# Mixture-of-experts phase of a fused layer on one core: the expert's conditional chunk taken last instead of first

## What is computed

```python
x = x + attention(layernorm(x))
x = x + moe(layernorm(x))

def moe(hidden_states, gate_w, w1, w2, w3):     # E=8 experts, K=2, H=256, F=896
    probs = softmax(hidden_states @ gate_w.T)
    # each token goes to its two best experts; an expert takes at most
    # capacity = 320 tokens of each of the 4 sequences: up to 1280 rows in all
    dispatch = einsum('bsm,bsec->ebcm', hidden_states, dispatch_mask)
    h1 = einsum('ebcm,emh->ebch', dispatch, w1)
    h3 = einsum('ebcm,emh->ebch', dispatch, w3)
    expert_out = einsum('ebch,ehm->ebcm', silu(h1) * h3, w2)
    return einsum('ebcm,bsec->bsm', expert_out, combine_mask)
```

## Time and profile before

| | us |
|---|---|
| median of 3 runs | 896.36 (894.65 to 896.64) |
| profiled execution, its own time | 896.49 |
| its span, first to last instruction | 894.8 |
| TensorE busy | 846.2 |
| VectorE, ScalarE, GpSimd busy | 472.9, 489.2, 467.1 |

### The profile page before, as it was taken

The page is one execution under the profiler, slowest core; times in us unless marked ns, Lnnn a source line. Parts: engine busy times, 40 slices in busy tenths (PEclk is TensorE's granted clock), DMA queues, the critical chain, the costliest instruction groups (busy, mean ns, idle before and its releaser), DMA issues. The chain is left out here.

```text
span 894.8 us, 18307 instructions
## 1 busy us (share of the span) xinstructions
PE 846.2 (95%) x6791; PEld 705.4 (79%) x6791; DVE 472.9 (53%) x1173; ACT 489.2 (55%) x876; POOL 467.1 (52%) x497
## 2 busy tenths in 40 slices
PE   3999999999999999889999999999999999999995
PEld 2777777777777777779889889879789889889885
DVE  6788788788888766343441442442351443342430
ACT  4578787777777779263542443443452444453331
POOL 4434766777767675564337355237346137447014
PEclk9999999999999999999999999999999999999998
DMA  5852132112111121546116236025417024314013
GB/s 154 320 193 67 50 102 67 62 56 80 38 38 38 38 98 53 170 150 139 42 42 118 86 92 111 5 78 89 112 48 137 22 72 92 82 42 54 7 19 42
DMA packets 50465, 73.93 MB, mean 83 GB/s; under 512 B 5056, under 2 KB 42176, under 8 KB 50368
## 3 DMA queue, kind: packets, MB, share of 16 engines
q1 hardware_dynamic: 35488, 53.46, 18.0%
q0 software_dynamic: 14592, 19.18, 12.5%
q10 hardware_dynamic: 288, 0.01, 0.0%
HBM read 38.41 MB, written 34.22 MB: 81 GB/s over the span
## 5 line engine op out<-in xcount | busy, mean ns | idle before, releaser
L1540 POOL TENSOR_TENSOR wlo<-wraw,whi 128x448 fp32r<-128x448 f32 x84 | 107.1, 1278 | 201.5 <-ACT whi L1597 201.5
L1817 PE MATMUL p<-xh,whi 128*128 128x512 f32 (+1 forms) x504 | 190.4, 378 | 7.3 <-DVE xl L1716 4.7
L1819 PE MATMUL p<-xh,wlo 128*128 128x512 f32 (+1 forms) x504 | 189.7, 376 | 0.0
L1818 PE MATMUL p<-xl,whi 128*128 128x512 f32 (+1 forms) x504 | 189.3, 376 | 0.0
L1734 DVE TENSOR_TENSOR hid<-gated,p 128x512 f32<-128x512 f32 (+1 forms) x126 | 81.1, 644 | 204.3 <-ACT gated L1611 204.3
L1548 POOL DMA_INDIRECT out<-ysb,index x80 | 126.0, 1575 | 85.2 <-ACT ysb L1633 55.1
L1611 ACT ACTIVATE gated<-p 128x512 f32<-128x512 f32 (+1 forms) x126 | 70.8, 562 | 179.7 <-PE p L1819 179.7
L1837 PE MATMUL py<-whi,hh 128*128 128x256 f32 x469 | 135.1, 288 | 6.2 <-DVE hl L1742 3.1
L1839 PE MATMUL py<-whi,hl 128*128 128x256 f32 x469 | 132.8, 283 | 0.0
L1838 PE MATMUL py<-wlo,hh 128*128 128x256 f32 x469 | 132.5, 283 | 0.0
L1817 PEld LDWEIGHTS p<-xh,whi 128*128 128x128 f32 x504 | 94.7, 188 | 27.4 <-DVE xl L1716 5.4
(11 more groups left out here) (192 smaller groups left out, 1441.1 us busy)
## 6 DMA issues: line engine op xcount, KB each, us to landing
wraw<-in_w SPq DMA_DIRECT2D x24, 896.0 KB
disp<-wraw SPq DMA_DIRECT2D x16, 662.5 KB, 9.2
xtok<-disp SPq DMA_DIRECT2D x16, 530.0 KB, 4.5
x_ring<-in_x SPq DMA_DIRECT2D x16, 256.0 KB, 3.0
out<-x SPq DMA_DIRECT2D x16, 256.0 KB
xtok<-disp SPq DMA_DIRECT2D x8, 265.0 KB, 6.1
out<-ysb,index POOLq DMA_INDIRECT x80
disp<-row,slot_i POOLq DMA_INDIRECT x64
```

The costliest lines, as they stand in the source:

```text
L1540: nc.gpsimd.tensor_tensor(wlo[e.const % 2][m][:, cut], wraw[k][:, cut], whi[e.const % 2][m][:, cut].bitcast(F32), ALU.subtract).then_inc(w ...
L1817: nc.tensor.matmul(dst[:, 0:w], hi[m][:, wcut], xh[xcut], start=(kt == 0), stop=False)
L1818: nc.tensor.matmul(dst[:, 0:w], hi[m][:, wcut], xl[xcut], start=False, stop=False)
L1819: ins = nc.tensor.matmul(dst[:, 0:w], lo[m][:, wcut], xh[xcut], start=False, stop=(kt == KT - 1))
```

## The change

`chunk_order` becomes 1, 2, 0 for experts 0 to 6 and 0, 1, 2 for expert 7, which keeps its old code under the name `last`. On TensorE `step` (now experts 1 to 6) is: `up` 1, then one branch on whether there is a rest. In its arm stand `turn` bank 4, `up` 2, `down` of chunk 1, `up` 0; in the other `up` 2 and `down` of chunk 1, between two passings-over. Then come `last_chunk` and `down_rest`. ScalarE and VectorE follow, so both arms there hold the second chunk's work as well. `first` has only three tiles' `down` ahead of the branch instead of four; the fourth follows `up` 2 inside the arms. On GpSimd the adds follow `tile_order`, so those of the rest come last, and the first of them waits for the adds of the expert's first five tiles.

```diff
 def chunk_order(e):
-    return [EARLY, *(c for c in range(NCH) if c != EARLY)] if e.reg is None and e.const == 0 else list(range(NCH))
+    return [1, 2, 0] if e.const < E - 1 else [0, 1, 2]
...
-    def run(eng, first, step):
+    def run(first, step, last):
         first(At(0))
-        step(At(1))
-        for e in range(2, E):
+        for e in range(1, E - 1):
             step(At(e))
+        last(At(E - 1))
...
         def add(e, t):
...
             pool.wait_ge(rows_in[0], 16)
+            if q == ST - REST and t < REST:
+                added_before(pool, e, ST // 2)
...
-            early = tile_order(e)[:CHUNKS[EARLY][1]]
+            early = tile_order(e)[:CHUNKS[EARLY][1] - 1]
...
-            for t in range(ST):
+            for q, t in enumerate(tile_order(e)):
                 add(e, t)
-                if t == ST - 3 and (e + 1).valid(E):
+                if q == ST - 3 and (e + 1).valid(E):
                     keep_index(e + 1)
...
     def on_scalar(act):
+        def with_rest_where_taken(e, between):
+            def hidden_rest():
+                turn_hi(e, TB - 1)
+                between()
+                hidden(e, 0, [])
+            def no_rest():
+                between()
+                n = chunk_at(e, 0) * FT
+                pass_over(act, e, (xh_ready, TB - 1, TB, 1), (gated_ready, n, HPE, FT), (hh_ready, n, HPE, FT))
+            where_taken(act, e, COMMON, hidden_rest, no_rest)
...
+        def step(e):
+            pieces = [(m, q) for m in range(3) for q in range(WP)]
+            half = pieces[FT - 1:]
+            hidden(e, 1, pieces[:FT - 1])
+            def second():
+                hidden(e, 2, list(half))
+                scale_chunk(e, 1)
+            with_rest_where_taken(e, second)
+            last_chunk(e, True)
+            scale_rest(e, 0)
...
     def on_vector(dve):
...
         def step(e):
+            hidden(e, 1)
+            with_rest_where_taken(e, lambda: hidden(e, 2))
+            next_rows(e + 1)
...
     def on_tensor(pe):
+        def with_rest_where_taken(e, between):
+            def up_rest():
+                turn(e, TB - 1)
+                between()
+                up(e, 0)
+            def no_rest():
+                pass_over(pe, e, (turned, TB - 1, TB, 1))
+                between()
+                pass_over(pe, e, (h_done, chunk_at(e, 0) * FT, HPE, FT))
+            where_taken(pe, e, COMMON, up_rest, no_rest)
...
         def first(e):
             t0, n = CHUNKS[EARLY]
-            for t in range(t0, t0 + n - 1):
+            for t in range(t0, t0 + n - 2):
                 down(e, t)
             for i in range(2, TB - 1):
                 turn(e, i)
-            down(e, t0 + n - 1)
+            down(e, t0 + n - 2)
             pe.wait_ge(taken_ready, 1)
-            rest_where_taken(e)
-            up(e, 2)
-            down_rest(e, 0)
+            def second():
+                up(e, 2)
+                down(e, t0 + n - 1)
+            with_rest_where_taken(e, second)
             last_chunk(e)
+            down_rest(e, 0)
         def step(e):
-            rest_where_taken(e)
             up(e, 1)
-            down_rest(e, 0)
-            up(e, 2)
-            down_chunk(e, 1)
+            def second():
+                up(e, 2)
+                down_chunk(e, 1)
+            with_rest_where_taken(e, second)
             last_chunk(e)
+            down_rest(e, 0)
```

More of the change, by code:

```diff
@@ L1519, in step @@
                 load_weights(nxt, 2)
-        run(sp, step, step)
+        run(step, step, step)
     def on_gpsimd(pool):
@@ L1578, in step @@
             added_before(pool, e, 0)
-            for t in range(ST):
+            for q, t in enumerate(tile_order(e)):
                 add(e, t)
-                if t == ST - 3 and (e + 1).valid(E):
+                if q == ST - 3 and (e + 1).valid(E):
                     keep_index(e + 1)
-        run(pool, first, step)
+        run(first, step, step)
         added_before(pool, At(E), 0)
@@ L1683, in first, with last @@
                 turn_hi(e, i)
-            scale_out(e, t0 + n - 1)
+            scale_out(e, t0 + n - 2)
             act.wait_ge(taken_ready, 1)
+            def second():
+                hidden(e, 2, [(m, q) for m in range(3) for q in range(WP)], 2)
+                scale_out(e, t0 + n - 1)
+            with_rest_where_taken(e, second)
[9 more added lines that the diff above has]
+            with_rest_where_taken(e, second)
+            last_chunk(e, True)
+            scale_rest(e, 0)
+        def last(e):
             rest_where_taken(e)
-            pieces = [(m, q) for m in range(3) for q in range(WP)]
-            hidden(e, 2, pieces, 2)
-            assert not pieces
+            hidden(e, 1, [])
             scale_rest(e, 0)
[L1691 to L1695, removed]
-            rest_where_taken(e)
[L1697 to L1700, removed]
+            hidden(e, 2, [])
             scale_chunk(e, 1)
-            last_chunk(e, more)
+            last_chunk(e, False)
         def free_hidden(eng, e, c):
@@ L1708, in free_hidden @@
             past.wait(eng, ffn_done, ST, tiles_done(past, q % NCH))
-        run(act, first, step)
+        run(first, step, last)
     def on_vector(dve):
@@ L1783, in step @@
             hidden(e, 2)
-            if (e + 1).valid(E):
-                next_rows(e + 1)
-        run(dve, first, step)
+        run(first, step, last)
     def on_tensor(pe):
@@ L1879, in first, with step, second, last @@
                 turn(e, i)
-            down(e, t0 + n - 1)
+            down(e, t0 + n - 2)
             pe.wait_ge(taken_ready, 1)
-            rest_where_taken(e)
-            up(e, 2)
-            down_rest(e, 0)
+            def second():
+                up(e, 2)
+                down(e, t0 + n - 1)
+            with_rest_where_taken(e, second)
+            last_chunk(e)
+            down_rest(e, 0)
+        def step(e):
+            up(e, 1)
+            def second():
+                up(e, 2)
+                down_chunk(e, 1)
+            with_rest_where_taken(e, second)
             last_chunk(e)
-        def step(e):
+            down_rest(e, 0)
+        def last(e):
             rest_where_taken(e)
@@ L1893, in step @@
             last_chunk(e)
-        run(pe, first, step)
+        run(first, step, last)
     return on_sync, on_gpsimd, on_scalar, on_vector, on_tensor
```

13 lines of the change are left out of this document (12 added, 1 removed).

## The result

The changed kernel takes 902.51 us (median of 7 runs, 901.23 to 904.88), the kernel before 896.64 beside it (7 runs, 894.65 to 899.86): a ratio of 1.0057, 95% interval 1.0038 to 1.0076. It is slower by some 5.9 us. I had forecast 891.8 with a range of 889.8 to 894.6; the time lies outside it, on the other side of no change.

What follows compares the result with a forecast made beforehand. TensorE, busy 95%, was taken as the bound, with about 10 us of waits to win. 4.7 + 0.3 + 2.6 - 2.2 - 0.9 = 4.5 us off 896.49 gave 892.0, stated as 891.8; 8-in-10 range 889.8 to 894.6.

Steps and rivals of the forecast that it cites:

- What bounds the kernel: Whole kernel: TensorE is busy 95% of the span, so the change can only win or lose its idle time.
- ten microseconds of stops are all there is to win: TensorE's waits from 360 us on total about 10 us; the whole forecast fails if its matmuls get slower.
- `xl`, +4.7: Experts 1, 3, 5: TensorE's stops for `xl` at the rest's `up` all go, hidden behind the second chunk; gain 4.7 us.
- expert 4's stop, +0.3: Expert 4's start: the 0.28 us wait for VectorE's passing-over ahead of `up` goes; gain 0.3 us.
- Expert 0, +2.6: Expert 0: chunk 2's first tile starts at 398.7 instead of 401.30 us; gain 2.6 us.
- The `hl` stop: Expert 0, ahead of chunk 2's first tile: TensorE's wait for VectorE's last `hl` falls from 3.1 to about 0.5 us.
- The wait for the rows: Expert 0, ahead of `turn`: a new wait of 0.5 us for chunk 2's rows, which the third tile covered before.
- The wait at each expert's end, -2.2: Ends of experts 0, 2, 4, 6: new wait for the last tile, 0.54 us each; cost 2.2 us.
- Expert 6 to 7, -0.9: Between experts 6 and 7: a second load, branch and passing-over with TensorE's queue empty; cost 0.9 us, bounds 0 and 1.4.
- VectorE, ScalarE, SyncE, GpSimd, 0: Other engines: new branches, later row and weight loads and later adds cost TensorE nothing; up to 0.3 us per expert in the range.
- The long jumps, slower: Rival: TensorE's jumps over 256 or 168 matmuls wait for code, 1.2 us in each of seven experts, 900.2 us; chance 0.08.

Runs made afterwards that it cites:

- short arms on TensorE: Changed kernel with the second chunk's work written once between two short branches, on TensorE alone, experts 0 to 6: 893.01 us, ratio 0.9938 to the kernel before.
- short arms on TensorE for expert 0: Changed kernel with the second chunk's work written once between two short branches, for expert 0 and TensorE alone: 896.68 us, ratio 0.9972 to the kernel before.
- short arms on all engines: Changed kernel with the second chunk's work written once between two short branches, on TensorE, ScalarE and VectorE: 876.11 us, ratio 0.9904 to the kernel before.
- the shifted kernel: Changed kernel plus 64 never-run matmuls in expert 0's inner rest arm, moving later code by 128 instructions: 903.99 us, ratio 1.0056 to the kernel before.
- the changed one once more: The changed kernel itself, unedited, measured again on the chip of its variants: 904.79 us, ratio 1.0068 to the kernel before.
- both with the empty queue: Changed kernel, and its version with short arms on TensorE, each waiting for the first `up` before the branch in experts 2, 4, 6: 906.35 and 880.22 us.

## Why the prediction was wrong, step by step

**What bounds the kernel.** Right: TensorE's idle time is all there was to win or lose. But the closing remark that "ten microseconds of stops are all there is to win" did not ask how much there was to lose.

**`xl`, +4.7; expert 4's stop, +0.3.** Right: none is left; what experts 2 and 4 show now, 0.37 and 0.23 at their second `up`, is left over from a load.

**Expert 0, +2.6.** The chain was right: from the first early tile to chunk 2's first tile the forecast has 398.7 - 364.71 = 34.0 us, and with short arms on TensorE it is 400.99 - 367.32 = 33.7. The `hl` stop was forecast at 0.5 and is 0.6. But the 36.6 us of before (401.30 - 364.71) hold 1.5 us of half clock under the early tiles, which I did not ask about. The wait for the rows was forecast at 0.5 from tiles that ran so slowly. It is 1.4 to 1.7 in the three executions of the new order whose early tiles ran at the full clock (the changed kernel, short arms on TensorE for expert 0 and for all), and none shows in the five where the clock was lower there (short arms on all engines, the shifted kernel, the changed one once more, both with the empty queue). With the half clock in both kernels the gain is 3.0 (36.6 against 384.00 - 350.45 = 33.6 in the last of these), without it in either 36.6 - 1.5 - 33.7 = 1.4.

```profile
384.00 0.39 PE L1881 MATMUL py<-whi,hh 128*128 128x256 f32 x1 [0.61 <-DVEq L1453]
```

In the changed kernel the stretch took 39.8: the jump's 4.7 and the half clock's 1.5 lie on top. This is the largest single miss.

**The wait at each expert's end, -2.2.** The nearest row's 0.54 holds where the expert has a rest; behind one without, it is 0.30. Three such ends cost 0.9 instead of 1.6.

**Expert 6 to 7, -0.9.** The sum was right, in part by luck: 0.54 + 0.9 = 1.44 was forecast for that stop, 1.45 measured. But expert 6 has no rest, and a wait behind such an expert is 0.30, so the second load and branch cost some 1.15 and not 0.9. By the Trainium skill's figures for the branch alone (Advanced Engine Details and Errata, Control Flow Timing) the stop would have been about 0.7, as an estimate; this trace speaks for the row that held the load and the waits too.

**VectorE, ScalarE, SyncE, GpSimd, 0.** Right: no wait of TensorE for `hid`; ScalarE shows no wait for weights from 410 us on; and the time from the last matmul to the end of the span is 9.6 us as against 9.5.

**The step that failed** is the one that gave TensorE's jumps no term in the sum. I had the distances (256 and 168 matmuls against 88), the size of the packets and the mechanism, as the rival "The long jumps, slower", and gave it 0.08. My reason was that the jumps of 88 are free. That says nothing about 168 or more when the mechanism is a step: the cost is zero within the block that is loaded and full beyond. The free row was read as evidence on a slope. The rival's 900.2 came near the 902.5, by luck: it put 1.2 us on each of seven experts, 8.4 in all, while three stops make 8.0. A load by itself costs 3.1 to 3.3. Experts 2, 4 and 6 jump the farthest and show only a stop of 0.37 or less. They jump behind a wide `up` whose queued matmuls last about as long as the load, and with that queue run dry each of them costs the 3.3 us too.

**In all,** the gains were 4.5 in the forecast. The kernel with short arms on TensorE gained 520.6 - 514.3 = 6.3 in that part of the span, of which 1.5 is the half clock of the one execution of before, so 4.8 by the order. Executions of equal clock say much the same: where the mean granted clock was 0.994 or 0.995, that kernel took 892.3 to 893.1 us and before 896.7 to 898.6 on the same chip. The changed kernel gained 3.2 of the 4.5, for the wait for the rows was 0.9 over the forecast, 0.6 of the hidden loads showed, and TensorE was busy 1.1 us longer, against 0.7 saved at the experts' ends; and the jumps took 8.0.

## What to carry to other kernels

Where an order needs a branch around much work, count the instructions that each arm makes the bottleneck engine jump over, a matmul as two, and ask whether the landing place is loaded. Work common to both arms belongs between two short branches: here that turned 0.6% slower into 0.6 to 1.0% faster with the same work in the same order. And when a cost has a threshold, a free instance below it is no evidence: price it at what lies beyond, or measure one. And before two traces are compared, look where each had its clock lowered: here 1.5 us of the 36.6 that the forecast for expert 0 started from were that.

## What the runs showed of the hardware

- TensorE's jump over 226 instructions cost nothing, the one over 290 cost 3.1 us with nothing queued. For a jump over 345 it depends on the place in the code: 128 instructions that never run moved stops of 1.5 to 1.8 us from experts 1 and 5 to expert 3.
- The load of a block costs 3.1 to 3.3 us with nothing queued in the quiet parts. In expert 0, amid other transfers (DMA share 0.82), the stop was 3.2 to 4.8 us though the branch follows a tile and no wait for it. From the packet's start to TensorE's next matmul it is 2.6 to 2.7 us each time; what holds the packet back for 0.6 to 2.1 us of the stop stays open.
- A stop of TensorE of 2 us or more was often followed by a stretch at 1.2 GHz, of 3.4 us (10.2 behind the longest stops), and sometimes not, at the same place in the same kernel. A stretch of 3.4 us adds about 1.5 us. Runs of one kernel differ along with it: before took 896.7 to 896.9 us at a mean granted clock of 0.995 and 900.0 to 902.2 at 0.988 or less, on one chip.
- A drain at an expert's end costs 0.30 us or 0.54, a drain with the load of a register and a branch behind it 1.2 to 1.45.
